# Second mixer: where GpSimd's three wide products of a quad stand among the row steps

## The reference, cut to what matters

```python
xBC = silu(conv(xBC) + b_conv)
x_inner, B_state, C_state = ...                  # 192 = 12 heads x 16, 16, 16
y, _ = ssd_minimal_discrete(x_inner * dt[..., None], A * dt, B_state, C_state, CHUNK)
y = y + x_inner * D_param[None, None, :, None]
y = (y - mu) * rsqrt(var + 1e-05) * gamma + beta
y = (y * silu(z)) @ W_out
```

## Time and profile before

| | |
|---|---|
| median of 3 executions | 2060.57 us (2054.01 to 2062.62) |
| profiled execution | 2070.34 us, its span 2068.5 us |
| PE, DVE, ACT, POOL busy in the span | 87%, 77%, 53%, 60% |
| second mixer | about 780 to 1650 us |
| there, 850 to 1600 us: PE, DVE, POOL busy | 718.87, 651.92, 442.44 of 750 us |
| mean granted clock there | 0.97 of 2.4 GHz |

### The profile page before, as it was taken

One profiled execution on the slowest core, in us unless ns is written; L12 is line 12 of the kernel. 1 busy time (PEld: TensorE's weight loads), 2 busy tenths in 40 slices (PEclk: granted clock), 3 DMA queues, 4 the chain that ended last, 5 costly groups with the idle time before them and its releaser, 6 DMA issues. The chain is left out here.

```text
span 2068.5 us, 63524 instructions
## 1 busy us (share of the span) xinstructions
PE 1791.5 (87%) x24986; PEld 1403.6 (68%) x24986; DVE 1588.6 (77%) x5061; ACT 1103.0 (53%) x2139; POOL 1238.0 (60%) x1313
## 2 busy tenths in 40 slices
PE   4884763888999949999998999999999959999996
PEld 3772642656777747777777777777777646777775
DVE  6885665966777866888989898988887669777774
ACT  2441411656777746555555554555543226777774
POOL 3337244675578744445476665667664547777776
PEclk9765755998999979999999999999998559999998
DMA  9310002455655662000000000000000025665553
GB/s 145 99 77 32 16 20 94 141 164 178 202 184 176 190 142 37 3 4 3 3 12 10 11 10 11 10 12 11 11 11 9 11 93 166 191 191 192 183 190 122
DMA packets 95404, 174.18 MB, mean 84 GB/s; under 512 B 53256, under 2 KB 66550, under 8 KB 95108
## 3 DMA queue, kind: packets, MB, share of 16 engines
q10 hardware_dynamic: 21312, 102.00, 15.2%
q1 hardware_dynamic: 56516, 41.86, 8.7%
q0 software_dynamic: 17280, 26.26, 3.7%
HBM read 134.71 MB, written 36.72 MB: 83 GB/s over the span
## 5 line engine op out<-in xcount | busy, mean ns | idle before, releaser
L1197 PE MATMUL ps<-rounded 97*128 97x512 f32 (+4 forms) x952 | 392.6, 412 | 19.7 <-DMA rounded<-weights_by_expert 8.0
L1198 PE MATMUL ps<-rounded 97*128 97x512 f32 (+4 forms) x952 | 373.0, 392 | 0.0
L1199 PE MATMUL ps<-rounded 97*128 97x512 f32 (+4 forms) x952 | 372.1, 391 | 0.0
L960 ACT ACTIVATE rounded<-ps 128x512 fp32r<-128x512 f32 (+1 forms) x444 | 259.8, 585 | 209.1 <-PE ps L1199 117.3
L2142 DVE TENSOR_TENSOR rounded<-arena,rounded 128x512 fp32r<-128x512 f32 (+1 forms) x321 | 248.7, 777 | 134.1 <-ACT arena L961 106.3
L1288 PE MATMUL ps<-rounded 128*128 128x464 f32 (+2 forms) x1428 | 320.7, 361 | 0.7 <-ACT rounded L980 0.6
L1288 PEld LDWEIGHTS ps<-rounded 128*128 128x128 f32 x1428 | 240.3, 200 | 51.3 <-issue 5.9
L961 ACT ACTIVATE arena<-ps 128x512 f32<-128x512 f32 (+1 forms) x444 | 260.3, 586 | 0.0
L779 POOL TENSOR_TENSOR w<-arena,consts 128x384 f32<-128x384 f32 x128 | 107.2, 838 | 243.2 <-issue 231.0
L1197 PEld LDWEIGHTS ps<-rounded 97*128 97x128 f32 (+2 forms) x952 | 169.5, 178 | 76.9 <-issue 15.0
L711 POOL TENSOR_TENSOR rounded<-arena,rounded 128x512 fp32r<-128x512 f32 (+1 forms) x123 | 154.3, 1254 | 100.8 <-ACT arena L961 94.8
(11 more groups left out here) (365 smaller groups left out, 3868.6 us busy)
## 6 DMA issues: line engine op xcount, KB each, us to landing
rounded<-weights_by_expert ACTq DMA_DIRECT2D x148, 673.0 KB
arena<-rows SPq DMA_DIRECT2D x68, 208.0 KB
residual<-in_x SPq DMA_DIRECT2D x16, 384.0 KB, 7.1
weights_by_expert<-rounded SPq DMA_DIRECT2D x8, 672.0 KB, 3.8
residual<-after_ffn SPq DMA_DIRECT2D x12, 384.0 KB, 6.6
w<-in_w SPq DMA_DIRECT2D x4, 576.0 KB
rows<-arena SPq DMA_DIRECT2D x11, 208.0 KB
after_ffn<-arena POOLq DMA_INDIRECT x142
```

The source lines that it names most:

```text
L960: act.activation(hidr[:, 0, c, 0:width(t)], bank(UPS[step % len(UPS)])[:, 0:width(t)], ACT.Gelu)
L1197: pe.matmul(dst, left[0], right[0], start=start, stop=False)
L1198: pe.matmul(dst, left[1], right[0], start=False, stop=False)
L1199: return pe.matmul(dst, left[0], right[1], start=False, stop=stop)
```

## The change

In POOL's step three products are moved, each to a later place; nothing is added or taken away, and the other engines' programs are the same:

```diff
                 if (c := quad(g, r, 5)) is not None:
                     steps_from(g, c, 1)
                     scaled(c, xdt, dt[:, c % 2, :, :], "xdt")
-                    pool.wait_ge(s["ex"], c + 1)
-                    ch.link(pool.tensor_tensor(wdt[:, :, :], dt[:, c % 2, :, :], ex3[:, c % 2, 1, :, :], ALU.mult))
-                    scaled(c, xw, wdt[:, :, :], "xw")
                 if (c := quad(g, r, 11)) is not None:
                     scale_and_bias(pool, ch, Q, c + 1, y_norm)
                 if (c := quad(g, r, 6)) is not None:
                     steps_from(g, c, 2)
+                    pool.wait_ge(s["ex"], c + 1)
+                    ch.link(pool.tensor_tensor(wdt[:, :, :], dt[:, c % 2, :, :], ex3[:, c % 2, 1, :, :], ALU.mult))
+                    scaled(c, xw, wdt[:, :, :], "xw")
+                if (c := quad(g, r, 7)) is not None:
                     scaled(c, xd, d_par.unsqueeze(1).to_broadcast([P, Q, NH]), "xd")
-                if (c := quad(g, r, 7)) is not None:
                     steps_from(g, c, 3)
```

## The result

The changed kernel is slower, by a little under 1%. Its median is 2079.2 us (2058.9 to 2096.7 in 19 executions), that of the kernel before, on the same chips, 2057.1 us (2044.4 to 2065.7 in 19). The ratio, which leaves out four disturbed executions of the changed kernel and none of the other, is 1.0085, with a 95% interval of 1.006 to 1.011: 12 to 23 us. The prediction had 2060 and a range of 2044 to 2076; 1.0085 times 2060.57 is 2078, just outside.

What follows compares the result with a forecast made beforehand. PE's waits for a DVE held by POOL's wide products were taken as the bound. Gains of 15.4 us and costs of 15.4 us summed to net 0: likeliest 2060 us, own range 2054 to 2066, 8 in 10 within 2044 to 2076.

Steps and rivals of the forecast that it cites:

- What bounds the kernel now: Second mixer: PE waits at L1270 for DVE's gate L1527, 23.7 us, as POOL's wide products hold DVE's small routing operations.
- L1610 and L1651: DVE's routing operations held by `xw`: freed by the change, gaining 1.31 us per held L1610 and 1.27 per held L1651.
- rival 3: POOL's power holds L1610 and L1651 0.95 us each, ten times: 9 us less gain, 2069; chance 0.05.
- L1614 and L1655: DVE is let in after the short `wdt`: L1614 gains 1.14 us; after L1655 a later small operation meets `xw`, +0.36 us.
- rival 2: DVE isn't let in between `wdt` and `xw`; L1614 and L1655 are held 1.85 us: +16 us, 2076; chance 0.22.
- Phase 7: Routing unit, r mod 4 = 3: L1631 held 1.57 and not 0.90 us; with L1474 and its followers, together +0.8 us.
- Phase 15: `xd` starts just ahead of L1474, holding L1474 and then L1478: DVE +2.1 us; 7.5 us over the units.
- The stalls that should follow in phase 1: PE waits at L1339 for L1436, 2.0 to 2.6 us; the slow clock behind them costs four times 1.7, 6.8 us.
- Phase 3, `xd` late: `xd` up to 0.3 us late for L1454 five times, 1.7 in the last quad: 0 to 3 us, taken as 0.
- The stall in phase 10: PE's wait at L1270 for DVE's gate in phase 10 of each routing unit stays near 3 us.
- net 0: Whole kernel: gains of 15.4 us in phases 4 to 10 against costs of 15.4 us, some 6 us to either side.
- slower: Measured time over 2070.9 us, from all of rival 2 and the upper half of rival 3; chance 0.25.

Runs made afterwards that it cites:

- e9: Changed kernel plus one wait on POOL ahead of its scatters until PE has done the scan of this step's row; 0.993 to the kernel before.
- e12: Kernel before with only the third product `xd` moved, plus a wait on POOL ahead of its scatters until PE's scan is done; 0.9931 to the kernel before.
- e6: Kernel before with the scatters issued at the head of POOL's step, the three products where they were; 0.9941 to the kernel before.
- e7: Changed kernel with all 96 scatters of the routing units issued behind POOL's last row step; 1.0377 to the kernel before, rows 1 to 112 727.3 us.
- e8: Kernel before with all 96 scatters of the routing units issued behind POOL's last row step; 1.0392 to the kernel before, rows 1 to 112 734.0 us.

## Why the prediction was wrong

Point by point, by its own steps.

- **What bounds the kernel now**: right as far as it went. L1270's waits for L1527 were the largest; the views that I read didn't show the rest, since L1356's 2.9 us of "issue" were a small line and I passed over it.
- **L1610 and L1651**: right, 0.16 and 0.17 us in all six units. The power L423 holds nobody: L1610 and L1651 ran wholly inside one in ten of twelve cases and took 0.16 to 0.17 us. So rival 3 is out. By the rule that the prediction quotes from the Trainium skill, page "SBUF — State Buffer", section "SBUF: two separate sides", it would have held them; the measurement decides.
- **L1614 and L1655**: right. L1614 took 0.28 us (0.35 forecast), and L1658 in the other place 1.48 in all six (1.5 forecast). DVE is let in behind the short product; rival 2's mechanism didn't happen. That the time came out near the 2076 of rival 2 is chance.
- **Phase 7**: L1631 took 1.57 us, as forecast, in four of six units (1.53 in a fifth).
- **Phase 15**: half right. In the second unit L1474 took 1.50 and L1475 0.85 us:

```profile
1158.57 1.51 POOL L785 TENSOR_TENSOR xn<-arena 128x768 f32<-128x768 f32 x1
1160.03 0.84 POOL L779 TENSOR_TENSOR w<-arena,consts 128x384 f32<-128x384 f32 x1
```

```profile
1158.64 1.50 DVE L1474 SCALAR_TENSOR_TENSOR arena<-arena 128x48 f32<-128x48 f32 x1
1160.06 0.85 DVE L1475 TENSOR_SCALAR arena<-arena 128x48 f32<-128x48 f32 x1
```

  I had the second hold at L1478; it fell on L1475. In the first and the third to fifth unit L1474 took 1.50, 0.87, 0.20 and 0.90. The stalls that should follow in phase 1 came twice, with 1.3 and 0.9 us at L1339 and not 2.0 to 2.6 four times, and no slow clock stands behind either. Only the first follows a held L1474 (first unit); the second is in the unit where L1474 took 0.20. In the second unit DVE's delay reached PE already in phase 15, at 1164.05, and behind it the clock fell for 6.8 us from 1165.9 on:

```profile
PE ps L1197 <- DVE residual L1536: 1.3, 1, 1.3
```

```profile
1164.00:1173.00 9.00, 8.96 (x143) 6.62 (x144) 8.49 (x41) 2.42 (x5) 2.06 (x3) 0.62 0.02 4
```

  So of this cost some 4.7 us came in the second unit (1.3 of waiting and half of 6.8), by another way than forecast, and 1.1 in the first. With 15.4 us in the sum it was the most oversized term.
- **Phase 3, `xd` late**: too low. DVE waited for it six times, 6.7 us (1.2 to 1.5 each in five quads, up to 0.3 forecast), where no such wait was before (DVE's waits, us in total, times, longest):

```profile
DVE arena L1454 <- POOL xn L785: 6.7, 6, 1.5
```

- **The stall in phase 10**, said to stay near 3 us: it was 0 to 2.1, in part because pauses had made PE late by then.
- **The sum of all this, net 0**: without scatters in the stage it came to -6.7 us in rows 1 to 112 and -3 in the times, about the edge of the forecast's own range of 6 to either side. With the wait in both orders it is some -10 us (0.995), with the scatters at the head of both steps +2 (0.995 against 0.9941). So the moved products alone are worth between nothing and a gain of some 10 us, depending on where the scatters stand, and none of the three shows a loss that is clear of the noise. Net 0 is near that, but as the sum of an oversized cost in phase 15 and an undersized one in phase 3, so in part by luck.
- **The step that failed** is one clause of the part on phase 15: "POOL's scatters now stand behind this too, and nobody waits for them in this stage." Nobody waits for them, but their issue itself stops PE where it meets the scan. I counted the scatters as POOL time and as data without a reader, and didn't ask what runs beside them. In its place, where the sum had nothing, the runs showed pauses of 16.0 us in rows 1 to 112 against 2.9 before, 13.7 us more for the scatters' presence in the changed order than in the one before (one profile each; some 20 us by the times), and 1.5% back for a wait that keeps most of them out of the scan.

A look at the kernel before could have warned: it has ten such pauses in this stretch, and at 1522.86 one stands 1.4 us behind a scatter's start, with a slow stretch of 6.8 us from 1524.6 on. I gave the case "slower" a chance of 0.25, for another reason.

## What to carry to other kernels

When an instruction is moved in a queue, list what moves with it in time though not in order, DMA issues above all, and look at what the other engines do in the new moment. An engine that issues nothing but small instructions is the one to check first. When a change takes away the wait that bound a kernel, each engine comes to run against the others at another offset; a second contention that the wait had kept apart can then cost as much as the wait did. The fastest orders here, e9, e12 and e6, were 0.6 to 0.7% faster than the kernel before, each with the scatters started at another place: e9 and e12 by moved products and one added wait, e6 by moving the scatters alone.

## What the runs showed of the hardware

- An indirect DMA that POOL issues (L807, 128 rows of 104 values) stops PE's stream of 32x16 matmuls twice, for up to 0.5 us each, with two to four matmuls between; PE resumes 0.5 to 0.8 and 1.3 to 1.5 us after its start. In the kernel before and the changed one the pauses stand where a scatter started between 0.4 us ahead of the scan's beginning and 2.5 us behind it. Where a scatter has only larger matmuls beside it in its first 1.5 us (L1288, L1342, L1378 and their like; 27 scatters in the changed kernel, 36 before), PE shows no idle time of this kind.
- It is the issue, not the moving of the data. For the scatters at 1120.65 and 1122.02 the two pauses of the first end at 1121.22 and 1121.98, and the DMA queues moved nothing until 1122.28. The views of DMA for 1120 to 1122 and for 1122 to 1123 (slices of 25 ns in the second):

```profile
DMA packets 0, 0.00 MB, mean 0 GB/s; under 512 B 0, under 2 KB 0, under 8 KB 0
```

```profile
DMA  0000000000069669640000000000000000000000
GB/s 0 0 0 0 0 0 0 0 0 0 0 266 532 266 266 399 266 134 0 0 0 0 0 0 0 0 0 0 0 0 0 0 0 0 0 0 0 0 0 0
DMA packets 32, 0.05 MB, mean 53 GB/s; under 512 B 16, under 2 KB 16, under 8 KB 32
```

- Nor is it POOL being busy: in e7 and e8 the wide products run beside the scans as before, and pauses are 0.5 us or less in rows 1 to 112. That one pause, at 1084.88 in e7, has no scatter near it, so a scatter isn't the only thing that can cause one. Which resource PE and the issue share I can't tell; no run tried it.
- DVE is let in between two products of POOL that are 0.08 us apart: L1614 waited for the short one and took 0.28 us in all, six times of six, where it had taken 1.49 behind the wide one.
